# Moving the first group's score pieces two token tiles earlier into the QKV projection, sorted by the last token tile they read

## The reference, cut to what matters

```python
x = x + 0.5 * ffn(layernorm(x))      # gate, up: 512 -> 1792; silu(gate) * up; down: 1792 -> 512
x = x + attn(layernorm(x))
x = x + 0.5 * ffn(layernorm(x))
# attn: qkv = h @ w_qkv.T + b_qkv; 32 query heads, 8 key/value heads of width 16;
#       rotary embedding on q and k; causal softmax (scale 1/16) over 1024 tokens; dense projection
```

## Time and profile before

| what | value |
|---|---|
| median of 3 runs | 1447.06 us (1446.97 to 1448.08) |
| the profiled execution's own time | 1447.79 us |
| its span (first to last instruction) | 1446.0 us |
| TensorE busy | 1373.3 us (95%) |
| VectorE busy | 1065.9 us (74%) |
| ScalarE busy | 608.1 us (42%) |
| GpSimd busy | 182.7 us (13%) |
| mean granted TensorE clock | 0.982 |

### The profile page before, as it was taken

One profiled execution on the slowest core, in us unless ns is written; L12 is line 12 of the kernel. 1 busy time (PEld: TensorE's weight loads), 2 busy tenths in 40 slices (PEclk: granted clock), 3 DMA queues, 4 the chain that ended last, 5 costly groups with the idle time before them and its releaser, 6 DMA issues.

```text
span 1446.0 us, 25511 instructions
## 1 busy us (share of the span) xinstructions
PE 1373.3 (95%) x9984; PEld 706.6 (49%) x9984; DVE 1065.9 (74%) x1611; ACT 608.1 (42%) x802; POOL 182.7 (13%) x269
## 2 busy tenths in 40 slices
PE   1999999999999988799999999999999999999998
PEld 0444444444444443233333333333577777777776
DVE  7999566865565589799999999965575666665544
ACT  4862223222211253378787877765222222222121
POOL 0000000000000354133333222211011011011000
PEclk8999999999999999699999999999999999999999
DMA  9703941011022021111111111030534746566440
GB/s 386 257 0 107 258 134 58 25 53 54 29 45 43 0 52 38 52 30 27 25 36 27 28 26 38 2 132 1 182 124 165 222 161 222 157 227 184 194 160 30
DMA packets 152028, 144.40 MB, mean 100 GB/s; under 512 B 129904, under 2 KB 133488, under 8 KB 148080
## 3 DMA queue, kind: packets, MB, share of 16 engines
q1 hardware_dynamic: 151920, 142.91, 31.5%
HBM read 96.73 MB, written 21.76 MB: 82 GB/s over the span
## 4 chain that ended last, share of the span: by engine, by line
PE 78%; DVE 13%; issue 3%; ACT 3%; SPq 2%; DMA 1%; POOL 0%; ACTq 0%; DVEq 0%
PE ps L2268 17%; PE ps L1816 15%; PE ps L2285 10%; PE ps L2042 10%; PE ps L1943 6%; PE ps L1837 6%; PE ps L2023 5%; PE ps L1863 3%; PE ps L2140 2%; PE ps L1933 2%; DVE rowmax L1549 1%; PE ps L2052 1%; DVE w_raw L1164 1%; DVE rowmax L1553 1%; DVE blocks L1453 1%
## 5 line engine op out<-in xcount | busy, mean ns | idle before, releaser
L980 ACT ACTIVATE probs<-ps 128x1024 f32<-128x1024 f32 (+3 forms) x384 | 292.5, 812 | 84.5 <-PE ps L2023 82.6
L1816 PE MATMUL ps<-xt_hi,w_all 128*128 128x512 f16 x896 | 275.3, 381 | 16.6 <-DVE w_all L1204 16.3
L2268 PE MATMUL ps<-xs,wpair 128*128 128x256 f16 x2352 | 261.3, 273 | 0.9 <-DVE second_sum L1701 0.9
L2268 PEld LDWEIGHTS ps<-xs,wpair 128*128 128x128 f16 x2352 | 230.1, 98 | 33.5 <-DVE second_sum L1701 1.1
L1549 DVE TENSOR_REDUCE rowmax<-ps 128x2 f32<-128x1024 f32 (+3 forms) x208 | 237.2, 1140 | 9.9 <-PE ps L1951 4.7
L1943 PE MATMUL ps<-ka,qa 48*128 48x512 f16 (+3 forms) x768 | 159.7, 341 | 21.0 <-DVE rowmax L1549 9.5
L1816 PE MATMUL ps<-xt_lo,w_all 128*128 128x512 f16 x448 | 170.8, 381 | 0.0
L2042 PE MATMUL ps<-probs,vs 128*32 128x512 f32 (+3 forms) x1536 | 165.2, 502 | 2.4 <-ACT ctx_sb L999 2.4
L1816 PEld LDWEIGHTS ps<-xt_hi,w_all 128*128 (+1 forms) x896 | 88.1, 98 | 125.0 <-issue 18.3
L1553 DVE TENSOR_REDUCE rowmax<-ps 128x1 f32<-128x512 f32 x192 | 131.0, 682 | 7.4 <-PE ps L1943 7.4
L2285 PE MATMUL ps<-wpair,hs_hi 128*128 128x512 f16 x448 | 133.3, 379 | 0.5 <-DVE hs_lo L1728 0.5
(11 more groups left out here) (168 smaller groups left out, 1815.6 us busy)
## 6 DMA issues: line engine op xcount, KB each, us to landing
wpair<-spill SPq DMA_DIRECT2D x28, 2304.0 KB, 8.7
spill<-block_parts SPq DMA_DIRECT2D x14, 512.0 KB, 2.7
spill<-w_all SPq DMA_DIRECT2D x24, 224.0 KB, 4.0
x<-x_in SPq DMA_DIRECT2D x4, 1024.0 KB, 5.3
wbase<-m1t SPq DMA_DIRECT2D x4, 896.0 KB, 12.1
w_raw<-w1t SPq DMA_DIRECT2D x4, 896.0 KB, 13.6
wbase<-m3t SPq DMA_DIRECT2D x4, 896.0 KB, 23.8
w_raw<-w3t SPq DMA_DIRECT2D x4, 896.0 KB, 24.1
```

The costliest lines, as they stand in the source:

```text
L980: nc.scalar.activation(probs[u % PBUF][:, 2 * pair:2 * pair + 2, 0:q1 - q0], wide(("scores", g, (u, pair)))[:, :, 0:q1 - q0], ACT.Exp, sca ...
L1816: last = mm(ps[:, bank, :], w[a][:, k, bass.ts(t, P)], xt[b][:, k, :], start=(k == 0 and n == 0), stop=(k == HB - 1 and n == 2))
L2268: last = mm(product_bank(n, i)[:, m, :], weight_of(n, m, a, weight, k), xs[c % 2][:, b, 2 * rows_ + k, :], start=(k == 0 and q == 0), stop ...
```

## The change

Group 0's pieces start at token tile 8 instead of 10. TensorE makes 23 of the 25 inside the projection (17 before), VectorE reduces all 25 in its tile loop (21 before). For group 0 alone the list is reordered: the sequence of pair and single stays, but within each kind the pieces are sorted by the last token tile that they read (`FIRST_PIECES`). Group 0's placement has a semaphore for each tile, and a piece waits only for the tiles it reads. The first piece is now a single piece on query tile 4, so it needs tiles 0 to 4. Last, `normal_parts(7, i - 3)` on VectorE moves from the head of iterations 3 to 6 to the place between `along(i)` and `low_parts(i-1)`.

```diff
-EARLY_TILE = 10
-EARLY_TAKEN = 3 * (TOKEN_TILES + 1 - EARLY_TILE)
-EARLY_MADE = EARLY_TAKEN - 4
+EARLY_TILE = 8
+EARLY_TAKEN = NP_
+EARLY_MADE = 3 * (TOKEN_TILES - EARLY_TILE) - 1
+
+def last_tile(piece):
+    return max(qt for qt, *_ in piece[1])
+
+def by_last_tile():
+
+    pairs = sorted((p for p in PIECES if p[0] == "pair"), key=last_tile)
+    singles = sorted((p for p in PIECES if p[0] != "pair"), key=last_tile)
+    return [(pairs if kind == "pair" else singles).pop(0) for kind, _ in PIECES]
+
+FIRST_PIECES = by_last_tile()
...
+    first_placed = [sem(f"first_placed{tt}") for tt in range(SEQ_TILES)]
...
     def placed(g):
-        return 16 * SEQ_TILES * (2 - g % 2) * (g // BUF + 1)
+        return 16 * SEQ_TILES * (2 - g % 2) * (g // BUF + (1 if g % BUF else 0))
...
         def place_operand_tile(g, tt):
+            placed_ = qk_placed[g % BUF] if g else first_placed[tt]
...
-                .then_inc(qk_placed[g % BUF], 16)
+                .then_inc(placed_, 16)
...
         def reduce_piece(k, r):
-            kind, parts = PIECES[r]
+            kind, parts = PIECES[r] if k else FIRST_PIECES[r]
...
         def early(i, at_):
-            if i >= EARLY_TILE:
+            if 0 <= 3 * (i - EARLY_TILE) + at_ < EARLY_TAKEN:
                 reduce_piece(0, 3 * (i - EARLY_TILE) + at_)
         for i in range(TOKEN_TILES + 1):
-            if 3 <= i < 7:
-                normal_parts(7, i - 3)
             if 1 <= i:
                 add_turned(i - 1)
             early(i, 0)
             if i < TOKEN_TILES:
                 along(i)
+            if 3 <= i < 7:
+                normal_parts(7, i - 3)
             early(i, 1)
...
         def score_piece(k, r):
-            kind, parts = PIECES[r]
-            if r == 0:
+            kind, parts = PIECES[r] if k else FIRST_PIECES[r]
+            if k == 0:
+                for tt in range(max([last_tile(p) + 1 for p in FIRST_PIECES[:r]], default=0), last_tile(FIRST_PIECES[r]) + 1):
+                    pe.wait_ge(first_placed[tt], 32)
+            elif r == 0:
                 pe.wait_ge(qk_placed[k % BUF], placed(k))
```

## The result

The changed kernel took 1449.94 us (median of 14 runs) beside 1447.88 us of the kernel before (14 runs on the same chip): ratio 1.0018, 95% interval [1.0011, 1.0025]. That is slower by some 2 us: clear of the noise, but its ratio lies inside the 0.2% that the prediction calls the same. The forecast was 1448.5. The profiled execution was the longest of the 14, 1454.76 us. The same kernel profiled again took 1450.03 us, its usual time, and its rows stand beside the first where the two differ. In the experiments they move by a few lines more. "The correction", here and in the expectations, is the first of these matmuls for group 0, L2023 or L2042: the start of `scores_t(0, 0, 0)`.

What follows compares the result with a forecast made beforehand. VectorE's maxima chain was taken to set `scores_t(0, 0, 0)`, with the `mrow` DMAs 1.0 us behind it. A start +1.6 us later, less piece 13's 0.20 us wait, gave +1.4 on 1447.06: 1448.5 us, range 1444.0 to 1451.0.

Steps and rivals of the forecast that it cites:

- Norm steps held: VectorE, iterations 3 to 6: moved steps held beside GpSimd's sine products, so 5.2 us an iteration against 5.4.
- The queue unchanged up to tile 4: SyncE's order unchanged, without pause: tile 4 lands 2.6 us later, at 528.3; TensorE stands 7.3 us before the first piece.
- Tile 15 later: ScalarE takes tile 15 out at 572.4 us, 2.7 later; TensorE resumes 8.7 earlier, two added tiles cost 11.4.
- its two waits: TensorE in the projection: 0.55 and 0.78 us where two singles or two pairs follow each other, coming two tiles earlier.
- the term: TensorE's half-clock stretch, ending inside 540 to 541 us: 0.6 us within the old five tile intervals of 30.4 us.
- The maxima chain at 593.3: VectorE starts group 1's reductions at 581.2, 2.7 us earlier; by that chain TensorE reaches `scores_t(0, 0, 0)` at 593.3.
- The wait for `mrow`: At `scores_t(0, 0, 0)`: SyncE's queue lands `mrow` at 597.5; TensorE stands from 593.3 to 597.6, starting 1.6 us later.
- From there to the end: Behind `scores_t(0, 0, 0)`: piece 13's 0.20 us reduction wait goes, and +1.4 us reaches the end.
- Not held: VectorE, iterations 3 to 6: moved steps run free, tile 4 lands at 527.0, 1447.2 us; chance 0.14.
- The maxima chain keeps setting the time: At `scores_t(0, 0, 0)`: `mrow` lands at 593.3, the chain's lead is kept, 1444.4 to 1442 us; chance 0.14.
- Slow rhythm and clock: TensorE behind the stop: longer half clock (+1.5 us), added tiles at 6.1 us (+0.8), 1449.3 to 1451 us; chance 0.20.

Runs made afterwards that it cites:

- experiment 1: Changed kernel with the norm steps put back at the head of iterations 3 to 6: 1447.55 us, ratio 0.9998.
- Experiment 3: Changed kernel with group 0's `mrow` DMAs ahead of group 3's transposes and the dense loads on SyncE: 1445.27 us, ratio 0.9976.
- experiment 4: Kernel before with group 0's `mrow` DMAs ahead of group 3's transposes and the dense loads on SyncE: 1448.12 us, ratio 1.0004.
- Kernel 10: Kernel before with only the norm steps moved, plus 24 unused matmuls of 384 columns ahead of tile 10's first piece: 1446.09 us, ratio 0.9985.
- kernel 11: Changed kernel with norm steps back at the head and group 0's `mrow` ahead of group 3's transposes: 1442.36 us, ratio 0.9958.
- experiment 6: Changed kernel with 36 unused matmuls of 384 columns ahead of the first piece: 1447.56 us, ratio 1.0001.
- kernel 2: Kernel before with only the norm steps moved behind `along`, pieces still from tile 10: 1451.71 us, ratio 1.0019.
- kernel 7: Changed kernel with tiles 0 to 4 ahead of the norm tiles and group 0's `mrow` ahead of group 3's transposes: 1444.54 us, ratio 0.997.
- kernel 9: Changed kernel with tiles 0 to 4 ahead of norm tiles, group 0's `mrow` ahead of group 3's transposes, 12 unused matmuls before the first piece: 1443.44 us, ratio 0.9965.
- kernel 5: Changed kernel with group 0's tiles 0 to 4 ahead of the first two norm tiles on SyncE: 1449.06 us, ratio 1.0005.
- Kernel 12: Changed kernel with norm steps at the head, `mrow` ahead of group 3's transposes, 36 unused 64-column matmuls before the first piece: 1441.60 us, ratio 0.9958.

## Why the prediction was right in its outcome, and what it had wrong

The forecast was +1.4 us on a median of 1447.06 us (3 runs). Over 14 runs the kernel before took 1447.88, so 0.8 of the 1.4 us between 1448.5 and 1449.94 is the base; the sum itself said +1.4 where the medians moved by +2.1.

**Norm steps held.** Right in kind. Scalar step and casts were lengthened as `low_parts` had been, and experiment 1 shows that this is where the later norm rows come from. The size was off: 5.4 us for an iteration on the mean instead of 5.2, up to 5.91, since the cast, which I let run free behind the second sine product (0.43 us), took 0.96 to 1.88. The trace of the kernel before already had a sign of this, which I overlooked: the scalar step of 0.92 us shown above, beside a fill on GpSimd. For the same reason the old interval wasn't 5.4 us throughout; that one was 5.8. In the longest case GpSimd's two fills of the padding stood behind the sine products and ended just ahead of it:

```profile
520.60 2.30 POOL L716 TENSOR_TENSOR rot_s<-qkv_raw,sin 128x320 f32<-128x320 f32 x2 [2.69 <-DVE rot L1534]
522.85 0.52 POOL L724 MEMSET parts_k<- 128x512 f16 x1
523.31 0.52 POOL L725 MEMSET parts_q<- 128x512 f16 x1
```

The fills end at 523.83 and the cast at 524.10; in the scalar step of before it was 509.84 and 510.12. The Trainium skill ("SBUF — State Buffer", section "Who interferes with whom") counts `tensor_scalar` and casts among the instructions that can meet GpSimd at the shared port; the trace agrees, with 1.09 for 0.55 us.

**The queue unchanged up to tile 4.** Right in its order: `qkv(8)` at 517.63 (517.3), the first piece reached at 521.37 (521.0), started at 527.79 (528.3), a stop of 6.4 us (7.3). The delay was mis-sized. The first norm tile's transpose went out 2.9 us later, not 2.6, yet tile 4's keys only 2.0 later, because in the kernel before one issue ahead of them had taken 2.12 us instead of 1.18, and the prediction carried that over:

```profile
521.14 2.12 SPq L528 DMA_TRANSPOSE qa<-parts_q  x1
```

**Tile 15 later.** 572.47 and 572.88 for 572.4, but by errors that cancel. The stop ended 0.5 us earlier than predicted. From tile 8 to tile 15 the prediction had 41.8 us, 0.6 of them for half clock; with the stop filled it was 40.58 (529.87 to 570.45), in the changed kernel 42.03 (530.44 to 572.47). So the tiles were 0.6 us quicker than the prediction's 5.7 each and its two waits made them, and the half clock took 0.9 more than the term had; the sum kept its old cost, and only a rival priced it at +1.5 above that. Another 0.3 lies ahead of tile 8's taking, 2.65 us behind the start of the first piece where before it was 2.34. Together -0.5, -0.6, +0.9 and +0.3 come to +0.1: the hit at tile 15 is luck.

**The maxima chain at 593.3.** Measured 593.31, and group 1's first reduction at 581.23 (581.2). Experiment 3 shows the chain alone, at 592.82.

**The wait for `mrow`.** Right in place and cause (experiments 3 and 4), with the landing mis-sized: from group 3's first transpose to the last `mrow` issue it was 13.3 us as before (580.80 to some 594.1, four issues in 2.53 us; 578.06 to 591.34), but that transfer landed 4.7 us later where the earlier trace rows gave 3.6. The changed kernel's own row (issues, KB each, median us to landing):

```profile
qa<-mrow SPq DMA_DIRECT2D x4, 4.0 KB, 4.4
```

So the correction came at 598.80, not 597.6: +2.84 for +1.6. Why this landing was longer the profile doesn't show.

**From there to the end.** The prediction carried +1.4 through. In the second execution the delay was 3.14 us at the correction and 1.79 at group 1's `mrow` copy: the step between the two took 17.01 us for 18.36. Windows of TensorE over this step (busy, granted clock, DMA share, GB/s), before:

```profile
595.96:614.32 18.36, 17.00 (x158) 0.73 0.01 1
```

and in the second execution:

```profile
599.10:616.11 17.01, 16.04 (x152) 0.80 0.01 1
```

Most of the gain is the clock. The half-clock stretch ended at nearly its old time (606.0 for 605.7), so of a step that began later it covered 6.9 us instead of 9.8, and TensorE was busy 0.96 us less. Its waits for reductions fell from 0.78 to 0.45 us, since VectorE had got ahead during the 5.4 us. Kernel 10 bears this out: no wait for `mrow`, 6.9 us at half clock behind its correction, and 17.22 us for the step. The prediction had given all this 0.20. Then a wait of 0.7 us for `mrow` at `scores_t(2, 0, 0)` came, where before there was none; the step from one `mrow` copy to the next that holds it took 25.24 us for 24.43, +0.8. 2.3 us reached the end of the span. The sizes missed were +1.5, -1.15 and +0.8, together +1.2; the other steps gave 0.3 back, which leaves the 0.9 between 1.4 and 2.3. So the gain between the two steps hid most of what the correction had been missed by.

**The rivals.** "Not held" is refuted by the 1.09. "The maxima chain keeps setting the time" is refuted for the change as made and is what experiments 3 and 11 bring about, at 1445.27 and 1442.36 us; 1442 was its far end. "Slow rhythm and clock" is right in half: the clock costs about 2 us by tile 15 (experiment 6), the rhythm nothing.

**Left open.** What decides whether the half-clock stretch that begins at 571 to 578 us ends at 599.5 to 606 or only at 616.5 to 619; between two executions of the changed kernel it differed by 13 us, worth some 4.7 us of time. Also why kernel 2's median has more of it than the kernel before.

## What to carry to other kernels

Starting a stage earlier was worth nothing here while the transfers behind it stayed where they were: follow the queue of each issuing engine to the next thing that is waited for, and put the small urgent transfers ahead of the large ones (four lines moved gave 4.7 us here, and nothing on the kernel before, whose bound lay elsewhere). Before moving VectorE work beside GpSimd's to fill a gap, look in the trace for what GpSimd does to it: here it was stretched until the gap was gone, and it delayed the rows that head the queue. Keep stops of TensorE short or filled: the price of a stop was its length and, often, half-speed work behind it.

## What the runs showed of the hardware that was not expected

**Matmuls of no use that save time.** With a stop of 6.4 us filled down to 1.2 us, the clock kept its upper level and tile 15 came 2.0 us earlier (kernel 6); with one of 4.4 us filled down to 0.4, the median fell from 1451.71 to 1446.09 us (kernel 10). Stops of 2.4 us (kernel 1) and 2.1 us (kernel 11) were followed by full clock; stops of 3.1 us (kernels 7 and 9) by 6.8 and 3.4 us at half, and one of 1.9 us (kernel 5) by 3.4 us, as was the 3.6 us stop of the kernel before. So the length of the stop alone doesn't decide it.

**`mrow` waits that go with instruction loads.** In the 13 profiles up to kernel 11 (before, changed, and the experiments) there are two places each, the `mrow` transfers of `scores_t(2, 0, 0)` and of `scores_t(10, 0, 0)`. Where a packet of the queue named "instruction" was recorded within 4.4 us of their issue, TensorE waited 0.4 to 1.2 us for them in 19 of 21 cases; in the 5 cases without one it never waited. Kernel 12, whose only purpose was to shift TensorE's instruction stream by 36 matmuls, had no such packet and no wait at either place. A packet alone isn't enough: at the other groups from 1 to 13 one fell within 4.4 us of the issue in 74 more cases in which TensorE didn't wait, and in one in which it did (0.6 us, kernel 6, group 8); kernel 9 has a wait of 0.2 us at group 4 without one. That the packet delays a transfer which is only just in time is what this suggests; it wasn't measured by itself.

**The same four 4 KB transfers** of group 0 took 3.9 to 4.4 us to land (medians) in the eight profiles in which they are issued just behind the loads into `wd_all` and `bd`, and 1.7 in five of the six in which they go ahead (kernels 3, 4, 7, 9 and 11; in kernel 12 it was 2.4).
